# One pass of slots per FFN in a macaron block: conditional slots last, second FFN in four routed stages

## The reference

```python
x = x + 0.5 * ffn(layernorm(x))
x = x + attn(layernorm(x))[encoder_out]
x = x + 0.5 * ffn(layernorm(x))

def ffn(x):                       # E = 8 experts, D = 256, F = 1024
    p = softmax(x @ Wr + br); gates = max(p); idx = argmax(p)
    xn = (x - mean) * rsqrt(var + 1e-5) * ln_g + ln_b
    h = relu(xn @ W1[idx] + b1[idx])
    return (h @ W2[idx] + b2[idx]) * gates

def attn(h):                      # 3 layers, 64 wide
    x = h @ down_w.T
    for i in range(3):            # conv of 4 taps, two gates, scan over the sequence, projection, rms norm
        x = recurrence_layer(x, ...)
    return x @ up_w.T
```

## Time and profile before

| | before |
|---|---|
| median of three runs | 807.17 us |
| the profiled execution: its time / its span | 813.11 / 811.4 us |
| mean granted PE clock in it | 0.942 |
| PE busy (matmul) | 679.7 us, 84% |
| DVE, ACT, POOL busy | 402.6, 263.8, 181.1 us |
| DMA | 126 MB, mean 155 GB/s |
| first product L1624, 2368 instructions | 294.7 us |
| second product L1638, 1184 instructions | 280.4 us |

### The profile page before, as it was taken

How to read it: one execution, slowest core, us unless ns; L and a number is a source line. 1 busy time by engine, 2 the same in 40 slices (tenths; PEclk the granted TensorE clock), 3 DMA queues, 4 the chain that set the end, 5 groups by cost and what they waited for, 6 DMA issues and landing times.

```text
span 811.4 us, 15300 instructions
## 1 busy us (share of the span) xinstructions
PE 679.7 (84%) x4346; PEld 594.4 (73%) x4346; DVE 402.6 (50%) x1377; ACT 263.8 (33%) x628; POOL 181.1 (22%) x186
## 2 busy tenths in 40 slices
PE   5319855999999999977995199998964899999995
PEld 4209755999997878866784178887863799999994
DVE  6526517333345677744785377883661233333321
ACT  3014211222225457524641068534120322222220
POOL 4521540011101111214225001025243011111111
PEclk9999967999999999999997599999997899999998
DMA  7998333565655452246102632335315354555520
GB/s 222 320 330 282 117 124 124 161 219 191 193 187 178 140 176 92 85 167 215 69 8 82 220 110 94 119 129 177 131 61 206 119 177 154 189 180 196 186 77 11
DMA packets 59784, 126.06 MB, mean 155 GB/s; under 512 B 8474, under 2 KB 36517, under 8 KB 59557
## 3 DMA queue, kind: packets, MB, share of 16 engines
q1 hardware_dynamic: 52628, 107.97, 39.5%
q0 software_dynamic: 7056, 16.93, 5.6%
HBM read 105.82 MB, written 21.53 MB: 157 GB/s over the span
## 4 chain that ended last, share of the span: by engine, by line
PE 66%; issue 10%; DVE 9%; DMA 4%; DVEq 4%; POOL 2%; another core or an unknown queue 2%; ACT 1%; SPq 1%; POOLq 0%; PEld 0%; PEldq 0%; ACTq 0%
PE bank L1624 27%; PE bank L1638 27%; PE bank L1534 2%; DMA pay<-routed_rows 2%; PE bank L1610 2%; PE bank L1474 1%; PE bank L1539 1%; DVE st L702 1%; POOL routed_rows L603 1%; PE bank L1489 1%; PE bank L1526 1%; PE bank L1565 1%; PE bank L1544 1%; DMA rb_all<-in_L_ffn_br 1%
## 5 line engine op out<-in xcount | busy, mean ns | idle before, releaser
L1624 PE MATMUL bank<-mn_t,w 128*128 128x128 f32 x2368 | 294.7, 283 | 9.8 <-DVE act_t L1108 8.5
L1624 PEld LDWEIGHTS bank<-mn_t,w 128*128 128x128 f32 x2368 | 286.3, 199 | 14.7 <-DVE act_t L1108 9.0
L1638 PE MATMUL bank<-w,act_t 128*128 x1184 | 280.4, 388 | 17.2 <-DVE res L1122 16.5
L1638 PEld LDWEIGHTS bank<-w,act_t 128*128 128x128 f32 x1184 | 222.7, 194 | 52.4 <-issue 24.7
L1347 ACT ACTIVATE mn_t<-bank,vec 128x128 f32<-128x128 f32 x148 | 59.6, 453 | 288.3 <-PE bank L1610 273.1
L1108 DVE TENSOR_SCALAR act_t<-bank,vec 128x128 f32<-128x128 f32 x296 | 83.5, 344 | 140.3 <-PE bank L1624 113.4
L1360 ACT ACTIVATE act_t<-bank,vec 128x128 f32<-128x128 f32 x296 | 84.5, 368 | 91.9 <-PE bank L1624 91.6
L1116 DVE TENSOR_TENSOR y_b<-bank,b_all 128x256 f32<-128x256 f32 x74 | 31.4, 424 | 122.8 <-PE bank L1638 114.2
L613 POOL DMA_INDIRECT out_x<-res,pay x37 | 36.9, 997 | 239.8 <-DVE res L1122 233.9
L613 POOL DMA_INDIRECT x_middle<-res,pay x37 | 37.8, 1021 | 227.9 <-DVE res L1122 225.4
L603 POOL DMA_INDIRECT routed_rows<-rows,dest x64 | 63.5, 993 | 46.3 <-DVE dest L802 29.2
(11 more groups left out here) (209 smaller groups left out, 456.7 us busy)
## 6 DMA issues: line engine op xcount, KB each, us to landing
w<-in_L_ffn_W SPq DMA_DIRECT2D x82, 1024.0 KB, 5.6
pay<-routed_rows SPq DMA_DIRECT2D x74, 130.0 KB, 2.2
rows<-in_L_attn_h SPq DMA_DIRECT2D x8, 512.0 KB, 9.1
rows<-x_middle SPq DMA_DIRECT2D x8, 512.0 KB, 5.1
routed_rows<-fill SPq DMA_DIRECT2D x2, 1040.0 KB, 8.1
b_all<-in_L_ffn_b SPq DMA_DIRECT2D x1, 1024.0 KB
routed_rows<-rows,dest POOLq DMA_INDIRECT x64
x_middle<-res,pay POOLq DMA_INDIRECT x37, 2.4
```

Source lines behind the costliest of these rows:

```text
L1624: last = t.matmul(b_hid[half][:, c % 4 * P:(c % 4 + 1) * P], w1[n % W1S][:, k * F + c * P:k * F + (c + 1) * P], mn_t[m][n % 2][:, k * P:(k ...
L1638: last = t.matmul(b_out[n % 2], act_t[n % 2][:, c * P:(c + 1) * P], w2[:, ds(eb * (WE // FC) + c * D, D)], start=c == 0, stop=c == FC - 1)
```

## The change

The two passes of an FFN become one. FFN 1 has 39 possible slots, FFN 2 44; 32 of each run always (`FIXED`), and the conditional rest stands at the end: in FFN 1 each engine tests `used > i` around its part of a slot, in FFN 2 the tests are nested (`tail`), so that an engine leaves at the first slot that is not used. There are no dummy stores, no counters stepped over at a start, and both FFNs have semaphores of their own.

A pass has stages with a table each (`EARLY`, `UPTO`): FFN 1 has 9 slots of chunks 0 and 1 and then the rest; FFN 2 has 4 slots of chunk 0, 9 of chunks 0 and 1, 8 of chunks 0 to 2, and the rest (up to 23). Ahead of the last stage only whole tiles of 128 rows are taken first, part-filled ones behind them. At a stage's first slot there is a gap of positions of its own; there PE, ACT and DVE wait for the table, and the input of that slot is prepared only then. SP waits for the table and the scatters when it loads the rows of a stage's first slot, four slots ahead.

`tables(f, s, part)` replaces the table functions and makes a table in six parts, placed by `TABLE_PARTS`. Chunks 2 and 3 of the input are loaded, transposed, turned and given moments ahead of slot 0; their `choose`, `place` and scatters come at slots 0 to 4. The second weights of experts 0 to 3 are loaded ahead; DVE works out in which slot each of the other four is first used (`order_of_use`), SP loads them in that order, between the first weights of slots 1 and 2, and PE waits for five to eight of them in its second products 0 to 3 instead of for all in slot 1. The lists of positions are new throughout.

```diff
-    SLOTS = (WITH[2], MOST[0] - JOINT, ALONE[1], MOST[1])
-    DYN = (0, MOST[0] - LEAST[0], 0, MOST[1] - LEAST[1])
+    EARLY = ((FULL,), (4, 9, 8))
+    UPTO = ((1, NC - 1), tuple(range(NC)))
+    LAST = [(T - t + PART) // P for t in TAKEN]
+    FIXED = (NT, NT)
+    SLOTS = [FIRST[p][-1] + LAST[p] for p in range(FFNS)]
...
-R_SCATTER = [[[None, None], [None, None], [49, 50], [51, 52]], [[840, 841], [936, 937], [1152, 1153], [1272, 1273]]]
-TABLES_ALONE = [None, 1920]
-TABLES_JOINT = [240, 2569]
+R_SCATTER = [[[None, None], [None, None], [24, 25], [96, 97]], [[744, 745], [1008, 1009], [1176, 1177], [1392,
+    1393]]]
+TABLE_PARTS = [[[None, None, None, None, None, None], [217, 240, 264, 336, 337, None]], [[1514, 1609, 1658, 1659,
+    1660, 1704], [2041, 2064, 2066, 2067, 2137, 2138], [2400, 2425, 2473, 2474, 2475, 2520], [2809, 2832, 2833,
+    2834, 2835, None]]]
...
+            def next_rows(p, i):
+                if i in FIRST[p]:
+
+                    s = FIRST[p].index(i)
+                    sp.wait_ge(s_tab, tables_at(p, s))
+                    for c in range(UPTO[p][s - 1] + 1 if s else 0, UPTO[p][s] + 1):
+                        of_sem = NTH * 16 if p == 0 else NJ * 16
+                        sp.wait_ge(routed_sem(p, c), of_sem)
+                slot_rows(p, i)
...
+            def between_passes():
+
+                used = slots_used(sp, 0)
+                for i in range(EARLY[1][0]):
+                    next_rows(1, i)
+                for u in range(FIXED[0], SLOTS[0] + 1):
+                    with sp.If(used == u):
+                        for i in range(W1S):
+
+                            last = max(j for j in range(u) if j % W1S == i)
+                            sp.wait_ge(m_h[0], 2 * last + 2)
+                            next_weights(1, i)
+                        results_stored(0, u)
+                load_x(1, NC - 1)
...
-            second_weights(range(0, E - 2))
+            load_x(0, 2)
+            second_weights(0)
+            load_parameters()
+            load_x(0, 3)
+            for e in range(1, EAGER):
+                second_weights(e)
             sp.wait_ge(s_tab, 1)
-            weights_from(0, 0)
-            sp.wait_ge(s_sc[0], 16 * NTH)
-            rows_from(0, 0)
-            second_weights(range(E - 2, E))
-            load_x(0, 2)
-            load_x(0, 3)
...
+            slot_weights(0, 0)
+            for i in range(RING - 1):
+                next_rows(0, i)
+            sp.wait_ge(s_order, 1)
+            for i in range(1, W1S):
+                second_weights_by_use(i - 1)
+                slot_weights(0, i)
+            for k in range(W1S - 1, LATER):
+                second_weights_by_use(k)
+
+            first_pass()
+            between_passes()
+            last_pass()
...
-            tables_alone(0)
+            for part in range(5):
+                tables(0, 0, part)
+            order_of_use()
+            tables(0, 0, 5)
             centre_down()
-            rows_done(0)
-            begin(0)
-            for p in range(PHASES - 1):
-                slots(p)
+            for c in range(HC, NC):
+                for b in range(NB):
+                    moments(R1, c, b)
+            norm(0, 0)
+            norm(0, 1)
+            first_pass()
             last_pass()
...
+            def begin_stage(p, i):
+
+                beside(8 * (PLACE[p][i] - 1))
+                pe.wait_ge(s_tab, tables_at(p, FIRST[p].index(i)))
+                turn_input(p, i)
+                if i:
+                    eb = second_expert(p, i - 1)
+                    for q in range(4):
+                        second_product(p, i - 1, q, eb)
+                        beside(8 * (PLACE[p][i] - 1) + 1 + q)
...
+                def tail(i):
+
+                    with pe.If(used == i):
+                        second_products(1, i - 1)
+                    if i < n:
+                        with pe.If(used > i):
+                            next_input(1, i + 1)
+                            for q in range(4):
+                                first_product(1, i, q)
+                            second_products(1, i - 1)
+                            tail(i + 1)
+
+                tail(FIXED[1])
```

More of the change, by code:

```diff
@@ L807, in keep_counts, with tables @@
                 dve.drain()
-            def slot_tables(r, kinds, n):
+            def tables(f, s, part):
+                n, upto = COUNT[f][s], UPTO[f][s]
+                last = s + 1 == len(COUNT[f])
+                c0 = 0 if f == 0 else upto
+                classes = upto + 1 - c0
+                kinds = classes + (1 if f and not last else 0)
                 m = kinds * E
-                rw, tb, of = (t[r % 2] for t in (tab_row, tab_b, tab_off))
+                i0 = FIRST[f][s]
+                rw, tb, of = (t[f][:, i0:i0 + n] for t in (tab_row, tab_b, tab_off))
                 large = m * n > SEG
@@ L1764, in _ @@
             counts(0, 0)
-            turn_logits(0, 1)
+            transposes(R1, 2, 0)
             ranks(0, 1)
+            transposes(R1, 2, 1)
             counts(0, 1)
+            logits(R1, 2)
+            turn_logits(0, 2)
+            for part in range(2):
+                transposes(R1, 3, part)
+            logits(R1, 3)
             parameters()
+            turn_logits(0, 3)
             pe.wait_ge(s_tpe, 2)
-            begin(0)
-            for p in range(PHASES - 1):
-                slots(p)
+            pe.wait_ge(s_tab, 1)
```

1135 lines of the change are left out of this document (514 added, 621 removed).

## The result

The kernel after takes 763.19 us (median of four runs, 758.71 to 765.87) beside 808.61 for the kernel before in the same series: ratio 0.943, 95% interval 0.938 to 0.949. The prediction was 744 with a range of 718 to 778, and faster at 0.95; sign and range held, and the time is 19 above the figure. In a later series, on another chip and in another condition of the machine, the same two kernels took 730.91 and 793.67, ratio 0.920 (0.917 to 0.923); what that condition is about is the subject of the experiments.

What follows compares the result with a forecast made beforehand. The kernel was taken as PE-bound with four holes. From a span of 811.4, 100.5 removed and 36.6 added gave 747.5; with 1.7 around it, 749.2, scaled to the median, 744 us (range 718 to 778).

Steps and rivals of the forecast that it cites:

- holes B and C: PE losses at the first FFN's end (34.6 us) and before the last pass (26.5); both were to go.
- (1) Early slots: Slots 0 to 8 of FFN 1: all 39.4 us of hole A goes, 5 comes back (bounds 2 and 14).
- hole A: Slots 0 to 6 before, 60.67 to 147.37 us: 39.4 excess, put down to routing work on PE, waits and half clock.
- (2) The start: Before the first product: added DVE work costs 1.7 us (bounds -3 and +6); second weights by use gain nothing.
- (3) The boundary of the FFNs: Between FFN 1 and FFN 2: 34.6 us of waiting goes, 11 of idle and cold clock comes (bounds 5.7 and 34.6).
- (4) Hole C: Before the last pass: the 26.5 us lost there go.
- (5) Stage starts: 2.3 us each at FFN 1 slot 9 and FFN 2 slots 13 and 21; 4 at FFN 2 slot 4.
- R4: Rival, chance 0.03: the five places waiting for a table are holes; slower from 17.2 us each, span 899 at 34.6 each.
- (6) Conditional slots: Conditional slots last: stepping over blocks in FFN 2 costs PE 1 us each, 5 in all (0 to 12.4).
- (7) Denser recurrence: Recurrence work beside 35 slots instead of 31: cost kept, +3 us for more places where an engine may wait.
- R2: Rival, chance 0.16: dependent chains; FFN boundary costs 25 instead of 11, crowded slots stretch by 0.5 each; 775 us.
- R1: Rival, chance 0.15: more gain, terms at early slots, FFN boundary, stage starts, skips and start fall to lower bounds; 721 us.

Runs made afterwards that it cites:

- u2: Kernel after with the table of FFN 1's second stage made in one piece in slot 4 again; 739.66 us, ratio 0.932 to before.
- e1_spread: Kernel after with the scatters beside slots mostly sent two per slot instead of in runs of eight; 733.12 us, ratio 0.903 to before.
- e5_best: e1_spread with chunk 3's moments moved behind the first two normalised tiles; 730.22 us, ratio 0.921 to before.
- after_again: Kernel after, unchanged, measured again beside before in a later series; 730.91 us beside 793.67, ratio 0.920.
- e2_fixed: Kernel after with the last five tiles of each FFN no longer conditional; 773.02 us, ratio 0.953 to before.
- e3_before_halves: Kernel before with its runs of scatters cut into fours in neighbouring slots; 788.29 us, ratio 0.994 to before.
- e4_after_halves: Kernel after with each run of eight scatters cut into two fours in neighbouring slots; 729.56 us, ratio 0.920 to before.
- p1: Kernel after with extra scatters and power instructions on POOL in otherwise undisturbed slots; eight scatters in a row cost PE 4.8 us, no kernel time given.

## Why the prediction was right, and where it was off

**What bounds the kernel, and the unit.** Right: 7.25 per slot wherever nothing is beside it, with 2368 and 1184 instructions. Of the holes B and C of the earlier trace rows C is gone and B is small (3).

**(1) Early slots: the step that failed.** I took all 39.4 of hole A for waits on POOL's stores and DVE's table and put 5 back. The table's part was right (u2: 8.8 for a predicted 8.5). But two runs of scatters stand in the new slots 3 and 5 as they stood in the hole, and what goes with them in PE's issue (these slots are 7.8 and 5.3 over pace in the trace of after) was not in my account at all: I priced a run as 10.2 us of POOL and asked only who waits for POOL. With the scatters spread, slots 0 to 8 without the stage start have an excess of 4.7; I had put 5. In after it was 14.5, just past my upper bound of 14, so 9.8 are the runs'. The sign I named, slot 9 near 135, came out at 144.5, and at 136.2 in e1_spread. In the quiet condition the excess is nearly as large (13.4) for another cause: slot 0 starts 7.7 earlier, DVE waits 6.0 for `pay` ahead of chunk 3's choice and PE 3.6 for that. e5_best shows that spreading doesn't cure it. The trace points at the loads: from 56 to 79 us the DMA engines are busy throughout (share 1.04 to 1.06, 368 to 390 GB/s), and the `pay` that DVE waits for was issued at 69.5 behind seven loads of weights issued since 54.1 and landed 9.0 later, where the page's median is 2.1. No run changes these loads in number, so this is not shown by experiment.

**(2) The start.** Right in size in this trace (62.0 for 62.4), but by luck: in the quiet condition the first product starts 7.7 earlier, since DVE's issue is not held up beside the first 16 scatters (no run spreads these). I had read such gaps in the earlier trace rows as "fetch gaps" and as given. The 7.7 buy nothing by themselves: product 9 starts at 137.3 in after_again and at 136.2 in e1_spread, whose first product starts only at 63.6. That second weights in order of use change no wait was wrong: without them PE waits 9.9. What they are worth in all, 3.3 by the medians, is not clear of the noise, so "nothing is gained" is not refuted.

**(3) The boundary of the FFNs.** Right. First products 36 and 37 are 29.2 apart (forecast about 25, 44.1 before), and the two slots together are 20.6 over pace. Of that 5.9 is idle and some 4 the half clock (5.71 for 3.74 in product 37, 3.78 for 1.9 in L1546), 10 for a predicted 11; the rest, 10.7, is side work, for some 7 forecast. The last waits in front are small, and the one for `mn` is the last, as forecast:

```profile
407.55 3.78 PE L1546 MATMUL bank<-rec,rec_t 128*128 128x512 f32 x4 [2.26 <-DVE rec L1023]
412.61 0.24 PE L1525 MATMUL bank<-chosen,tri 128*128 128x64 bf16 x1 [1.28 <-DVE sums L797]
...
413.46 0.66 PE L1618 MATMUL bank<-ident,mn 128*128 128x128 f32 x2 [0.56 <-DVE mn L1127]
```

**(4) Hole C.** Right: nothing is left at that place.

**(5) Stage starts.** Right: 2.7, 1.8 and 4.4 at slots 9, 50 and 58 (2.3 each forecast), about 6.5 at FFN 2's slot 4 (4 forecast), side work taken off. R4, the way to a slower kernel, needed 17.2 at each.

**(6) Conditional slots.** Wrong by 5, on the dear side: the five slots take 7.25 each. The Trainium skill, page "Runtime: NRT & Kernel Launch", section "Instruction fetch mechanics", says that a taken branch stalls for a fetch where its target is not in the current two pages. The trace agrees with the reading that these short skips stay inside, with 0.00 for each; no run measures how far they reach. The end is 11.1 for 8.6 before, which e2_fixed shows is not the tail's doing: it is 11.1 with those five slots unconditional too, and 11.8 in e3_before_halves with the code of before.

**(7) Denser recurrence.** The stretch behind slot 9 shows no such wait outside the slots beside runs; the longest there, 4.49 in slot 45 of after and over the 4 that I had named as a sign, is absent from after_again. The +3 was not needed. From product 9 to the last one I had 604.0, the quiet condition has 580.9 and the trace of after 606.3. Below my figure lie the skips (5), two runs of scatters in slots 33 and 46 of before that I had kept without knowing (19.56 and 15.90 there, 13.29 and 10.26 in e3_before_halves: 11.9), and some 6 more, the +3 among them, of which I can't name the rest. Above the quiet one lie the runs beside slots 31, 38, 45 and 53 of after, 22.9 by comparison with after_again, and 2.5 of other differences.

So the sum was near in part by luck, because errors met: 9.8 too little for slots 0 to 8, 11 too little for the runs behind them, 2.5 for other differences there and 2.5 at the end, against 5 too much for skips and some 6 elsewhere. As a ratio, 744 to 807.17 is 0.922, which is what the quiet condition gives (0.920), though the sum knew nothing of conditions; the 0.943 of the disturbed one lies between it and R2's 0.960. R1's 721, a ratio of 0.893, was met in neither.

## What to carry to other kernels

Ask of a long run on one queue not only who waits for it but what the rows of the other engines look like beside it: "issue" gaps between single instructions and "remote" releasers on several engines at once had one cause here, not many. Break runs of indirect scatters into twos, one slot each, even where POOL has the time: in the disturbed condition it was worth 30 us (4%), and in the quiet one e5_best, which has the twos, lost nothing. Fours lost nothing in the quiet condition; in the disturbed one only the probes speak for them. Look as well whether the trace has all its semaphore records before a delay is put down to the hardware. And run the kernel before beside every variant: without its 811.8 and 793.6 I would have taken e4_after_halves for the better of two cures.

## What I had not expected of the hardware

In one condition of the machine, while every execution was recorded, eight indirect scatters of 128 rows of 1040 bytes back to back (10.2 us) delayed other engines from about the fifth on: PE issued single matmuls 0.7 to 1.4 us apart, and signals of finished matmuls arrived up to 8.4 us late (8.6 in p1). Beside the 16 of the start DVE operations of 0.2 us came with gaps of 1.0 to 2.4. The cost to PE was 4.8 and 5.0 in slots with nothing else beside them. Four in a row cost 0. In the other condition eight cost 0 as well, with the same spacing of 1.28 on POOL. In the first condition most of the scatters' landing records were missing (226 of 1024 and more in after), in the other next to none. And a power instruction on POOL between scatters had an idle of 8.6 and 9.5 behind it that no row explains.
